# Second attention in another order of quarters, and the convolution's taps moved beside the expert gathers

## The chip, the cores and the metric

One Trainium2 chip, one core. The metric is the device time of one execution in microseconds (us); lower is better. "Before" is the kernel as it stands, "after" the same kernel with the change below.

## The reference, cut to what matters

Two decoder layers on x of 4 batches x 512 tokens x 256 features, float32: attention, cross attention and experts, then again attention, cross attention with modulation, and experts, each with a residual sum and a layer norm.

```python
x = _layernorm(x + _L0_attn_ref(x, ...), axis=-1)
x = _layernorm(x + _L0_xattn_ref(ctx_768, x, ...), axis=-1)
x = _layernorm(x + _L0_ffn_ref(x, L0_ffn_Wr, L0_ffn_W1, L0_ffn_W2), axis=-1)
x = _layernorm(x + _L1_attn_ref(x, ..., L1_attn_pre_proj, L1_attn_post_proj, L1_attn_mem_k, L1_attn_mem_v, ...), axis=-1)
x = _layernorm(x + _L1_xattn_ref(x, ctx_768, ..., L1_xattn_log_dt, L1_xattn_A_re, ...), axis=-1)
x = _layernorm(x + _L1_ffn_ref(x, ...), axis=-1)
```

Two parts are touched. The second attention is causal, has 16 heads and 16 memory keys, mixes its scores over the heads with a 16x16 matrix, keeps of every row of mixed scores only the 64 largest, takes the softmax of them, and mixes over the heads again. The second cross attention holds a state-space convolution, whose kernel ("taps", 512 values for each of 256 channels) depends on weights alone and is computed long before it is used.

## The kernel before, in words

The program is a sequence of blocks; in each, the five engines have instruction streams written out by hand, and wait for one another by semaphores.

**First experts, `l0_experts`.** 39 slots of 128 sorted token rows. For each slot PE makes the hidden values (`hidden`, L1453), transposes the rows of a later slot (L1442) and makes the output (`out`, L1464). DVE copies the slot's first weights (`bring`) and between these computes a piece of the factors of the convolution kernel, `K.V` (32 values a channel) and `K.U` (16 a channel). Four slots make a chunk of 32 channels, 8 chunks in all. Once a chunk, behind `out` of its second slot, PE multiplies the chunk's factors (`taps`, L1473, 32 products of 32x16, tile `f_pk`), and DVE copies the result to `K.taps` in four copies (L1543).

**Combination and norm, `l0_combine_and_norm`.** POOL issues 32 indirect gathers of expert outputs (L2846), eight for each batch. For each batch DVE adds them to x with their gates, takes moments, waits for ACT's root (`root`, L2888) and normalizes x; PE transposes x (`turn`, L2867) and ACT copies it to xT (L2894). Between, PE multiplies the taps with a Fourier matrix in eight steps (`transform`, L2856), each of which ACT copies out (`keep`, L2883); SP stores the eight at the end. Before, the order on PE is four transforms, turn of batch 0, four transforms, turns of batches 1 to 3, and ACT follows it.

**Second attention, `l1_attention`.** The queries of a batch fall into four groups of 128 (quarters); 16 groups in all. Quarter i sees 16 + 128(i + 1) keys at most. `ORDER` says in what order a batch's quarters are worked through. A group is 16 tiles of 8 queries x 16 heads = 128 rows, and two tiles are a pair: 8 pairs a group, 128 pairs in all, numbered k below. Tile r of quarter i is 16 + 128 i + 8(r + 1) wide, so pairs are 24 and 32 wide at the start of the first quarter and 520 and 528 at the end of the fourth. For each pair:

- PE mixes the rows over the heads (`mix`, L1874, tile `a_pmix`); ACT copies that to `mixed` (L1999); POOL adds the causal cut (L2118);
- DVE searches the 64 largest of each row (L2176 to L2260), for a wide row in two halves; its last step signals `found`;
- POOL compares the rows with the 64th value and adds the penalty (`a_probs`, L2141 and L2149); ACT takes the exponentials (L2018) and then the negated maximum of the next pair (`negated`, L2006, `a_negmax`), for which DVE waits before the pair after that;
- DVE inverts the sums (L2215), POOL scales the second mixing matrix (L2102, `a_kp`), and PE multiplies with it in chunks of 128 keys (`post`, L1883, `a_pat`). A tile of over four chunks takes both PSUM banks of `pat`, so that its successor waits for ACT's copies (L2029, L2033). Only the last pair of the fourth quarter has five chunks.

Iteration k of PE is: `mix` of pair k + 2, side work, `post` of pair k - 2, and the products with the values (`heads`, L1901 and L1905, and `output`, L1916) of the group before. ACT's iteration is the copies of mixed scores of pair k + 1, exponentials of k - 1, negated maxima of k, side work, the copies behind `post`, and those of the products. The side work (`l1_units`) hangs on the place of a group in its batch, not on the quarter: at the first place of batch 0 the scores of the group at the second place; at the second place the values (pairs 0 and 1), the scores of the third (pairs 2 to 4) and of the fourth place (pairs 5 to 7, in 3, 3 and 2 units); at the third and fourth place the queries, keys and scores of the next batch. One unit of scores is two heads (L1864, `a_psc`) for one group. A row of over 512 scores is cut in halves of 264, so a unit is four fills of a PSUM bank for the fourth quarter and two for any other (`l1_fills`).

Of the kernel before, what the change touches and what calls it, by code (L numbers as in the profile page):

```python
# [15 lines left out]
B, S, D = 4, 512, 256  # L16
# [945 lines left out]
LO, HI = 32, 16  # L962
MAGIC = 1.5 * 2 ** 23
TWO_PI = 6.283185
CHUNKS = 8
CW = D // CHUNKS
# [409 lines left out]
def l0_experts(nc, G, R, K):  # L1376

    with ExitStack() as ctx:
        sb, ps, sem = buffers(nc, ctx, "f0")
# [10 lines left out]
        px = ps("px", [P, KD, P])  # L1390
        ph = [ps(f"ph{i}", [P, 512]) for i in range(2)]
        py = [ps(f"py{i}", [P, D]) for i in range(2)]
        pk = ps("pk", [LO, CW, HI])
        tapped, taps_read = sem("tapped"), sem("taps_read")
        made = K.steps[0]
        xs_loaded = [sem(f"xs_loaded{i}") for i in range(3)]
        w2_loaded = [sem(f"w2_loaded{i}") for i in range(2)]
        y_stored = [sem(f"y_stored{i}") for i in range(3)]
# [3 lines left out]
        with nc.Block() as block:  # L1402
# [32 lines left out]
            @block.tensor  # L1435
            def _(pe):
                def turn_rows(j):
                    pe.wait_ge(xs_loaded[j % 3], 16 * (j // 3 + 1))
                    if j >= 1:
                        pe.wait_ge(x_ready, j)  # L1440
                    for k in range(KD):
                        ins = pe.transpose(px[:, k, :], xs[:, j % 3, k * P:(k + 1) * P], G.ident[:])  # L1442
                    ins.then_inc(x_turned, 1)

                def hidden(j):
                    pe.wait_ge(x_ready, j + 1)
                    for half in range(2):
                        if j >= 1:
                            pe.wait_ge(h_done, 2 * (j - 1) + half + 1)
                        pe.wait_ge(w1_brought, 2 * j + half + 1)  # L1450
                        for f in range(HF):
                            for k in range(KD):
                                ins = pe.matmul(ph[half][:, f * P:(f + 1) * P], first[half][:, k, f * P:(f + 1) * P], xsT[:, j % 2, k, :],  # L1453
                                                start=(k == 0), stop=(k == KD - 1))
                        ins.then_inc(h_full, 1)

                def out(j):
                    pe.wait_ge(w2_loaded[j % 2], 16 * (j // 2 + 1))
                    if j >= 2:
                        pe.wait_ge(y_done, j - 1)  # L1460
                    for f in range(FT):
                        if f % HF == 0:
                            pe.wait_ge(h_done, 2 * j + f // HF + 1)
                        ins = pe.matmul(py[j % 2][:], hT[j % 2][:, f * P:(f + 1) * P], w2[:, j % 2, f, :],  # L1464
                                        start=(f == 0), stop=(f == FT - 1))
                    ins.then_inc(y_full, 1)

                def taps(c):
                    pe.wait_ge(K.dve_steps, made + K.STEPS * (c + 1))
                    if c >= 1:  # L1470
                        pe.wait_ge(taps_read, c)
                    for i in range(CW):
                        ins = pe.matmul(pk[:, i, :], K.V[:, CW * c + i, :], K.U[:, CW * c + i, :], start=True, stop=True)  # L1473
                    ins.then_inc(tapped, 1)

                turn_rows(0)
                turn_rows(1)
                hidden(0)
                for j in range(SLOTS):
                    if j + 1 < SLOTS:  # L1480
                        hidden(j + 1)
                    if j + 2 < SLOTS:
                        turn_rows(j + 2)
                    out(j)
                    if j % K.PIECES == 1 and 1 <= j // K.PIECES <= CHUNKS:
                        taps(j // K.PIECES - 1)

            @block.scalar
            def _(act):
# [34 lines left out]
            @block.vector  # L1524
            def _(dve):
                def bring(j):
                    e = dve.value_load(R.expert[0:1, j:j + 1], min_val=0, max_val=E0 - 1)
                    for half in range(2):
                        if j >= 1:
                            dve.wait_ge(h_full, 2 * (j - 1) + half + 1)  # L1530
                        w = R.w1[:, bass.ds(e, 1), :, half * 512:half * 512 + 512].rearrange("p a k f -> p (a k) f")
                        dve.tensor_copy(first[half], w).then_inc(w1_brought, 1)

                dve.wait_ge(R.w1_loaded, 16 * E0)
                bring(0)
                for j in range(SLOTS):
                    if j + 1 < SLOTS:
                        bring(j + 1)
                    c = j // K.PIECES - 1
                    if j % K.PIECES == 3 and 0 <= c < CHUNKS:  # L1540
                        dve.wait_ge(tapped, c + 1)
                        for a in range(4):
                            ins = dve.tensor_copy(K.taps[32 * a:32 * a + 32, :, CW * c:CW * c + CW],  # L1543
                                                  pk[:, :, :].rearrange("l c (j a) -> l a j c", a=4)[:, a])
                        ins.then_inc(taps_read, 1)
                    if 0 <= (j - 1) // K.PIECES < CHUNKS:
                        K.piece(dve, (j - 1) // K.PIECES, (j - 1) % K.PIECES)

# [8 lines left out]
GONE = -3e38  # L1557


ORDER = (0, 3, 1, 2)  # L1560
KEYS1 = MEM + S
KK1 = INNER1 // P
CH1 = KEYS1 // P + 1
# [1259 lines left out]
def l0_combine_and_norm(nc, G, R, K):  # L2823

    with ExitStack() as ctx:
# [4 lines left out]
        rstd = sb("rstd", [P, TT])  # L2830
        pf = [ps(f"pf{i}", [P, 512]) for i in range(2)]
        pT = [ps(f"pT{i}", [P, NT, P]) for i in range(2)]
        dft_in, spectrum, kept, stored = sem("dft_in"), sem("spectrum"), sem("kept"), sem("stored")
        moments, rooted, x_ready = sem("moments"), sem("rooted"), sem("x_ready")
        turned, copied, dve_steps = sem("turned"), sem("copied"), sem("dve_steps")
# [5 lines left out]
        with nc.Block() as block:  # L2841
# [9 lines left out]
            def _(pe):  # L2851
# [8 lines left out]
                def turn(b):  # L2860
                    pe.wait_ge(x_ready, NT * (b + 1))
                    for k in range(KD):
                        n = b * KD + k
                        if n >= 2:
                            pe.wait_ge(copied, n - 1)
                        for q in range(NT):
                            ins = pe.transpose(pT[n % 2][:, q, :], G.x[:, b * NT + q, k * P:(k + 1) * P], G.ident[:])  # L2867
                        ins.then_inc(turned, 1)

                pe.wait_ge(dft_in, 16)  # L2870
                for m in range(FT):
                    transform(m)
                turn(0)
                for m in range(FT, 2 * FT):
                    transform(m)
                for b in range(1, B):
                    turn(b)

            @block.scalar
            def _(act):  # L2880
# [9 lines left out]
                def copies(b):  # L2890
                    for k in range(KD):
# [2 lines left out]
                        act.copy(G.xT[:, k, b * S:(b + 1) * S], pT[n % 2][:].rearrange("p a b -> p (a b)")  # L2894
                                 ).then_inc(copied, 1)

                for m in range(FT):
                    keep(m)
                root(0)
                copies(0)  # L2900
                for m in range(FT, 2 * FT):
                    keep(m)
                for b in range(1, B):
                    root(b)
                    copies(b)

# [592 lines left out]
```

## Time and profile before

| | |
|---|---|
| median of 3 runs | 3562.75 us (3560.17 to 3565.22) |
| the profiled execution | 3564.6 us, span 3562.8 us |
| PE busy | 2771.1 us (78%) |
| DVE busy | 2386.4 us (67%) |
| ACT, POOL busy | 1118.4 us, 997.6 us |
| mean granted TensorE clock | 0.823 |

How to read it: the profile covers one execution. The busy share is an average over blocks with different limits; it doesn't tell what a block waits for. PE's clock is granted in two levels, 1.2 and 2.4 GHz, shown as 0.50 and 1.00 of full speed; a number between is a mean over a stretch. Every float32 product shows as two records, so a count of records is twice the count of products. The experts' block runs from 672 to 977 us of the span, the combination to 1032, the second attention to 2586.

### The profile page before, as it was taken

What the parts mean: (1) busy time and instruction counts of PE and PEld (TensorE: products, weight loads), DVE (VectorE), ACT (ScalarE), POOL (GpSimd) and SP (SyncE); (2) the same over time, 40 slices, a digit from 0 to 9 for tenths busy, and PEclk for the clock granted to TensorE, in tenths of its full rate; (3) what the DMA queues carried; (4) which work ended last, traced back from release to release, by engine and by line L of the source; (5) the groups of instructions that cost most, each with busy time, mean ns of one, the idle gap of its engine ahead of it and who ended that gap; (6) DMA issues with size and microseconds to landing.
All of it is one profiled execution on the core that took longest, in us unless ns stands there. A gap on an engine that the chain in (4) does not pass through costs nothing. (4 is left out here: it accounts for less than half of the span.)

```text
span 3562.8 us, 43681 instructions
## 1 busy us (share of the span) xinstructions
PE 2771.1 (78%) x12600; PEld 1905.2 (53%) x12600; DVE 2386.4 (67%) x8897; ACT 1118.4 (31%) x2893; POOL 997.6 (28%) x1242
## 2 busy tenths in 40 slices
PE   4665995499957667767787668765479999999999
PEld 2223564499834345535464445454436656666666
DVE  4996565466334999899989998999767635212112
ACT  1113562244313333433343334332232123222221
POOL 2552000300032454545454545455312210000000
PEclk7556996699976788787867886867679999999999
DMA  2000002455532211212122211111020032212212
GB/s 96 0 0 14 6 1 104 129 170 164 162 131 92 76 59 63 65 65 69 54 72 68 69 55 67 60 54 35 1 93 1 1 89 67 79 53 63 77 51 68
DMA packets 180780, 235.56 MB, mean 66 GB/s; under 512 B 35761, under 2 KB 138869, under 8 KB 180286
## 3 DMA queue, kind: packets, MB, share of 16 engines
q1 hardware_dynamic: 177470, 224.37, 19.7%
q0 software_dynamic: 3072, 8.39, 0.7%
q8 instruction: 103, 1.69, 0.2%
q14 instruction: 135, 1.11, 0.1%
HBM read 170.57 MB, written 62.13 MB: 65 GB/s over the span
## 5 line engine op out<-in xcount | busy, mean ns | idle before, releaser
L1883 PE MATMUL a_pat<-a_kp,a_probs 128*128 128x128 f32 x1344 | 292.8, 392 | 237.7 <-POOL a_kp L2102 232.7
L1883 PEld LDWEIGHTS a_pat<-a_kp,a_probs 128*128 128x128 f32 x1344 | 259.6, 288 | 317.3 <-POOL a_kp L2102 300.0
L2141 POOL TENSOR_SCALAR a_probs<-a_mixed,a_best 128x120 f32<-128x120 f32 (+12 forms) x208 | 302.4, 1454 | 251.8 <-DVE a_best L2208 115.8
L3408 DVE TENSOR_TENSOR tl_hT<-tl_act_out,tl_gate 128x512 f32<-128x512 f32 x128 | 88.6, 692 | 385.8 <-ACT tl_act_out L3279 385.8
L1864 PE MATMUL a_psc<-a_kT,branch 64*128 64x264 f32 (+3 forms) x640 | 225.6, 603 | 119.5 <-ACT a_stage L1966 118.8
L2194 DVE MAX8 a_best<-a_rest 128x8 f32<-128x208 f32 (+23 forms) x768 | 271.2, 374 | 0.0
L2248 DVE MATCH_REPLACE8 a_rest<-a_best,a_rest 128x104 f32<-128x104 f32 (+31 forms) x732 | 266.0, 373 | 0.0
L2102 POOL TENSOR_SCALAR a_kp<-a_kpost,a_rden 128x128 f32<-128x128 f32 x256 | 152.9, 609 | 386.2 <-DVE a_rden L2215 385.8
L1874 PE MATMUL a_pmix<-a_rows,a_kpre 128*128 128x264 f32 (+41 forms) x528 | 185.8, 482 | 84.2 <-ACT a_mixed L1999 79.7
L2186 DVE MATCH_REPLACE8 a_rest<-a_best,a_rest 128x204 f32<-128x204 f32 (+23 forms) x672 | 245.9, 371 | 0.0
L2256 DVE MAX8 a_best<-a_rest 128x8 f32<-128x104 f32 (+31 forms) x732 | 244.6, 377 | 0.0
L3193 PE MATMUL tl_py<-tl_w,tl_hT 128*128 128x256 f32 x1024 | 241.6, 379 | 0.0
L3174 PE MATMUL tl_ph<-xT,tl_w 128*128 128x512 f32 x512 | 240.7, 592 | 0.0
L3193 PEld LDWEIGHTS tl_py<-tl_w,tl_hT 128*128 128x128 f32 x1024 | 194.6, 190 | 80.2 <-issue 60.0
L1864 PEld LDWEIGHTS a_psc<-a_kT,branch 64*128 64x128 f32 x640 | 118.0, 257 | 212.2 <-ACT a_stage L1966 185.9
L2018 ACT ACTIVATE a_probs<-a_probs,a_negmax 128x72 f32<-128x72 f32 (+28 forms) x232 | 126.1, 545 | 262.4 <-POOL a_probs L2149 259.8
L3279 ACT ACTIVATE tl_act_out<-tl_ph,tl_b 128x512 f32<-128x512 f32 x128 | 88.0, 688 | 351.8 <-PE tl_ph L3174 351.8
L2149 POOL TENSOR_TENSOR a_probs<-a_mixed,a_probs 128x72 f32<-128x72 f32 (+28 forms) x232 | 185.3, 820 | 9.3
L1874 PEld LDWEIGHTS a_pmix<-a_rows,a_kpre 128*128 128x128 f32 x528 | 100.3, 226 | 126.1 <-issue 116.1
L1966 ACT COPY a_stage<-a_psc 128x264 f32<-128x264 f32 (+3 forms) x320 | 112.7, 381 | 121.9 <-PE a_psc L1864 115.7
L1453 PE MATMUL f_ph<-f_xsT,xT 128*128 128x128 f32 x1248 | 148.6, 278 | 0.0
L1453 PEld LDWEIGHTS f_ph<-f_xsT,xT 128*128 128x128 f32 x1248 | 147.0, 195 | 1.7
(465 smaller groups left out, 5643.1 us busy)
## 6 DMA issues: line engine op xcount, KB each, us to landing
f_w<-in_L_ffn_W SPq DMA_DIRECT2D x39, 1024.0 KB, 5.7
tl_gate<-l_gates SPq DMA_DIRECT2D x256, 128.0 KB, 2.9
l_scores<-a_stage SPq DMA_DIRECT2D x32, 528.0 KB, 2.7
l_scores<-a_stage SPq DMA_DIRECT2D x32, 400.0 KB, 2.4
l_scores<-a_stage SPq DMA_DIRECT2D x32, 272.0 KB, 2.1
f0o_w<-in_L_ffn_W SPq DMA_DIRECT2D x8, 1024.0 KB, 12.9
sorted_x<-z_blank SPq DMA_DIRECT2D x1, 4992.0 KB, 15.6
f_xs<-sorted_x SPq DMA_DIRECT2D x39, 128.0 KB, 5.3
```

The lines of the kernel that those rows point to most:

```text
L1453: ins = pe.matmul(ph[half][:, f * P:(f + 1) * P], first[half][:, k, f * P:(f + 1) * P], xsT[:, j % 2, k, :], start=(k == 0), stop=(k == KD ...
L1864: full(pe.matmul(out[:, 0:hi - lo], qT[r, j, i * P:(i + 1) * P], kT[r, j, lo:hi], start=True, stop=True))
L1874: ins = pe.matmul(pmix[:, at, 0:hi - lo], kpre[:], rows[:, g % 4, lo:hi], start=True, stop=True)
L1883: ins = pe.matmul(pat[:, at + c, :], probs[:, g % 4, c * P:(c + 1) * P], kp[:, g % 4, :], start=True, stop=True)
L2141: ins = pool.tensor_scalar(p, x, best[:, a, LAST, 7:8], HIDE, ALU.is_lt, ALU.mult)
L2149: pool.tensor_tensor(p, x, p, ALU.add).then_inc(masked, 1)
L2186: last[a, part] = signal(dve.match_replace(values, top, values, GONE))
L2194: ins = dve.max(best[:, a, q, :] if part == 0 else low[:, a, 8 * q + 1:8 * q + 9], values)
L2248: last[a] = signal(dve.match_replace(rest[:, a, 0:wd], best[:, a, q - 1, :], rows_of[a] if q == 1 else rest[:, a, 0:wd], GONE))
L2256: last[a] = signal(dve.max(best[:, a, q, :], rest[:, a, 0:wd]))
L3174: ins = pe.matmul(ph[m % 2][:], lhsT, G.xT[:, k, b * S:(b + 1) * S], start=(k == 0), stop=(k == KD - 1))
L3193: ins = pe.matmul(py[t][:, 0:D], src[:, t * P:(t + 1) * P], w, start=(n == 0), stop=False)
```

## The change

`ORDER` gets the second and the fourth entry swapped. The groups of every batch are now worked through as quarters 0, 2, 1, 3 and not 0, 3, 1, 2. All that is derived from it (widths, stores, fetches, the number of fills of a unit) follows; the places' side work stays. The products of the taps leave the experts' slots and become the first work of PE in the combination's block, with two PSUM tiles in turn; the copies move from DVE to ACT, ahead of the first root. Behind them, PE's order is turn of batch 0, four transforms, turn of batch 1, four transforms, turns 2 and 3; ACT's is the same.

```diff
 l0_experts:
-                def taps(c):
-                    pe.wait_ge(K.dve_steps, made + K.STEPS * (c + 1))
-                    if c >= 1:
-                        pe.wait_ge(taps_read, c)
-                    for i in range(CW):
-                        ins = pe.matmul(pk[:, i, :], K.V[:, CW * c + i, :], K.U[:, CW * c + i, :], start=True, stop=True)
-                    ins.then_inc(tapped, 1)
...
-                    if j % K.PIECES == 1 and 1 <= j // K.PIECES <= CHUNKS:
-                        taps(j // K.PIECES - 1)
...
-                    if j % K.PIECES == 3 and 0 <= c < CHUNKS:
-                        dve.wait_ge(tapped, c + 1)
-                        for a in range(4):
-                            ins = dve.tensor_copy(K.taps[32 * a:32 * a + 32, :, CW * c:CW * c + CW],
-                                                  pk[:, :, :].rearrange("l c (j a) -> l a j c", a=4)[:, a])
-                        ins.then_inc(taps_read, 1)
...
-ORDER = (0, 3, 1, 2)
+ORDER = (0, 2, 1, 3)
...
 l0_combine_and_norm, PE:
+                for c in range(CHUNKS):
+                    if c >= 2:
+                        pe.wait_ge(taps_read, c - 1)
+                    for i in range(CW):
+                        ins = pe.matmul(pk[c % 2][:, i, :], K.V[:, CW * c + i, :], K.U[:, CW * c + i, :], start=True, stop=True)
+                    ins.then_inc(tapped, 1)
+                turn(0)
                 pe.wait_ge(dft_in, 16)
+                pe.wait_ge(taps_read, CHUNKS)
                 for m in range(FT):
                     transform(m)
-                turn(0)
+                turn(1)
                 for m in range(FT, 2 * FT):
                     transform(m)
-                for b in range(1, B):
+                for b in range(2, B):
                     turn(b)
...
 l0_combine_and_norm, ACT:
+                for c in range(CHUNKS):
+                    act.wait_ge(tapped, c + 1)
+                    for a in range(4):
+                        ins = act.copy(K.taps[32 * a:32 * a + 32, :, CW * c:CW * c + CW],
+                                       pk[c % 2][:, :, :].rearrange("l c (j a) -> l a j c", a=4)[:, a])
+                    ins.then_inc(taps_read, 1)
+                root(0)
+                copies(0)
                 for m in range(FT):
                     keep(m)
-                root(0)
-                copies(0)
+                root(1)
+                copies(1)
                 for m in range(FT, 2 * FT):
                     keep(m)
-                for b in range(1, B):
+                for b in range(2, B):
```

The combination's block on ACT, before (`cn_pf` is the transform's PSUM tile, `cn_std` the root, `f0o_w` holds the spectrum):

```order
L2879 UNCONDITIONAL_BRANCH
L2883 COPY f0o_w<-cn_pf 128x256 x4
L2888 ACT_TABLE_LOAD
L2888 ACTIVATE cn_std<-cn_rstd 128x4
L2894 COPY xT<-cn_pT 128x512 x2
L2883 COPY f0o_w<-cn_pf 128x256 x4
L2888 ACTIVATE cn_std<-cn_rstd 128x4
```

and after (`cn_pk` is the taps' PSUM tile):

```order
L2869 UNCONDITIONAL_BRANCH
L2890 COPY f0o_taps<-cn_pk 32x4x32 x32
L2878 ACT_TABLE_LOAD
L2878 ACTIVATE cn_std<-cn_rstd 128x4
L2884 COPY xT<-cn_pT 128x512 x2
L2873 COPY f0o_w<-cn_pf 128x256 x4
L2878 ACTIVATE cn_std<-cn_rstd 128x4
L2884 COPY xT<-cn_pT 128x512 x2
L2873 COPY f0o_w<-cn_pf 128x256 x4
L2878 ACTIVATE cn_std<-cn_rstd 128x4
```

32 copies stand ahead of the first root, and the last four copies of the spectrum now stand ahead of the third root, where they stood ahead of the second.

PE in the second attention where one batch ends and the next begins, before (the last pair of the batch's last group, then the first pairs of the next batch):

```order
L1874 MATMUL a_pmix<-a_rows,a_kpre 128x56
L1874 MATMUL a_pmix<-a_rows,a_kpre 128x64
L1883 MATMUL a_pat<-a_kp,a_probs 128x128 x6
L1874 MATMUL a_pmix<-a_rows,a_kpre 128x72
L1874 MATMUL a_pmix<-a_rows,a_kpre 128x80
L1883 MATMUL a_pat<-a_kp,a_probs 128x128 x8
L1901 MATMUL a_pO<-a_aT_large,a_v 64x128 x6
L1905 MATMUL a_pO<-a_edge,a_v 64x16 x2
```

and after:

```order
L1854 MATMUL a_pmix<-a_rows,a_kpre 128x56
L1854 MATMUL a_pmix<-a_rows,a_kpre 128x64
L1863 MATMUL a_pat<-a_kp,a_probs 128x128 x8
L1854 MATMUL a_pmix<-a_rows,a_kpre 128x72
L1854 MATMUL a_pmix<-a_rows,a_kpre 128x80
L1863 MATMUL a_pat<-a_kp,a_probs 128x128 x10
L1881 MATMUL a_pO<-a_aT_large,a_v 64x128 x8
L1885 MATMUL a_pO<-a_edge,a_v 64x16 x2
```

The narrow mixes of the new batch now stand beside 8 and 10 chunk products and not 6 and 8, and each two heads take 8 products with the values and not 6.

PE at the second place of a batch, pairs 5 and 6, after; the side work there (`a_psc`) is now 12 fills of 264 for each pair, where before it was 6 fills of 400:

```order
L1844 MATMUL a_psc<-a_kT,branch 128x264 x12
L1863 MATMUL a_pat<-a_kp,a_probs 128x128 x6
L1896 MATMUL a_pO<-a_wo,a_cT 128x256 x8
L1897 MATMUL a_pO<-a_bo,a_ones 128x256
L1898 MATMUL a_pO<-x,ident 128x256
L1854 MATMUL a_pmix<-a_rows,a_kpre 128x168
L1854 MATMUL a_pmix<-a_rows,a_kpre 128x176
L1844 MATMUL a_psc<-a_kT,branch 128x264 x8
```

## Rows read from the trace of the kernel before

**Rows 1.** Stretches of the second attention: length, DVE busy, granted clock, DMA
```profile
1086.00:1128.00 42.00, 6.74 (x48) 0.50 0.33 118
1128.00:1468.80 340.80, 338.10 (x1545) 0.77 0.20 66
1468.80:1488.00 19.20, 3.14 (x25) 0.71 0.15 41
```

**Rows 2.** Timeline of the experts: start, duration, engine, work, idle before
```profile
722.35 2.20 PE L1473 MATMUL f_pk<-branch,sk_V 128*32 128x16 f32 x64
...
726.68 0.69 DVE L1532 COPY xT<-f0o_w 128x1024 f32 x1 [4.63 <-PE f_ph L1453]
...
731.83 3.73 PE L1453 MATMUL f_ph<-f_xsT,xT 128*128 128x128 f32 x32
...
739.07 3.73 PE L1453 MATMUL f_ph<-f_xsT,xT 128*128 128x128 f32 x32
...
753.66 2.20 PE L1473 MATMUL f_pk<-branch,sk_V 128*32 128x16 f32 x64
```

**Rows 3.** Timeline of the combination's block
```profile
998.57 0.21 ACT L2888 ACTIVATE cn_std<-cn_rstd 128x4 f32<-128x4 f32 x1
...
1001.61 8.76 PE L2856 MATMUL cn_pf<-f0o_taps,f0o_w 128*128 128x256 f32 x32
...
1017.89 0.20 ACT L2888 ACTIVATE cn_std<-cn_rstd 128x4 f32<-128x4 f32 x1 [3.56 <-DVE cn_rstd L2925]
...
1021.89 3.38 DVE L2916 SCALAR_TENSOR_TENSOR x<-f0o_w,f0o_gates,x 128x256 f32<-128x256 f32 x8 [2.09 <-DMA f0o_w<-sorted_y,f0o_slot]
```

**Rows 4.** Timeline of the second attention's start
```profile
1117.03 7.37 PE L1864 MATMUL a_psc<-a_kT,branch 64*128 64x264 f32 x16
```

**Rows 5.** Timeline, scores of the third quarter at the second place
```profile
1620.50 2.09 PE L1864 MATMUL a_psc<-a_kT,branch 64*128 64x400 f32 x4 [0.63 <-ACT a_stage L1966]
1622.84 2.09 PE L1864 MATMUL a_psc<-a_kT,branch 64*128 64x400 f32 x4 [0.24 <-ACT a_stage L1966]
```

**Rows 6.** Timeline from the third quarter's last search (batch 0) into the next batch
```profile
1468.92 3.32 POOL L2141 TENSOR_SCALAR a_probs<-a_mixed,a_best 128x392 f32<-128x392 f32 x2 [2.81 <-DVE a_best L2208]
...
1472.32 2.00 POOL L2149 TENSOR_TENSOR a_probs<-a_mixed,a_probs 128x392 f32<-128x392 f32 x2
...
1475.26 0.31 DVE L2235 MAX8 a_best<-a_mixed 128x8 f32<-128x40 f32 x2 [6.16 <-ACT a_negmax L2006]
1475.28 2.93 PE L1883 MATMUL a_pat<-a_kp,a_probs 128*128 128x128 f32 x12 [4.01 <-POOL a_kp L2102]
...
1479.74 0.35 DVE L2235 MAX8 a_best<-a_mixed 128x8 f32<-128x56 f32 x2 [4.11 <-ACT a_negmax L2006]
1479.93 3.64 PE L1883 MATMUL a_pat<-a_kp,a_probs 128*128 128x128 f32 x16
...
1485.32 0.23 DVE L2232 TENSOR_REDUCE a_least<-a_mixed 128x1 f32<-128x72 f32 x1 [5.17 <-ACT a_negmax L2006]
```

**Rows 7.** Timeline behind the fourth quarter's last search, batch 1
```profile
1648.22 4.18 POOL L2141 TENSOR_SCALAR a_probs<-a_mixed,a_best 128x520 f32<-128x520 f32 x2 [3.62 <-DVE a_best L2208]
...
1652.48 2.55 POOL L2149 TENSOR_TENSOR a_probs<-a_mixed,a_probs 128x520 f32<-128x520 f32 x2
...
1668.26 1.35 PE L1883 MATMUL a_pat<-a_kp,a_probs 128*128 128x128 f32 x10 [0.94 <-ACT a_edge L2033]
...
1670.13 0.27 ACT L2033 COPY a_edge<-a_pat 128x128 f32<-128x128 f32 x1
```

**Rows 8.** Stretches, as in rows 1: batch 1's fourth, second and third quarter
```profile
1511.10:1648.10 137.00, 135.60 (x585) 0.75 0.20 70
1648.10:1724.70 76.60, 75.78 (x362) 0.83 0.15 44
1724.70:1833.20 108.50, 107.78 (x474) 0.77 0.22 76
```

**Rows 9.** Timeline of the second attention's end
```profile
2566.95 5.85 PE L1883 MATMUL a_pat<-a_kp,a_probs 128*128 128x128 f32 x28 [6.46 <-POOL a_kp L2102]
...
2573.54 0.88 PE L1901 MATMUL a_pO<-a_aT_large,a_v 128*64 128x128 f32 x12 [0.74 <-ACT a_edge L2033]
```

More of the change, by code:

```diff
@@ L1392, in l0_experts @@
         py = [ps(f"py{i}", [P, D]) for i in range(2)]
-        pk = ps("pk", [LO, CW, HI])
-        tapped, taps_read = sem("tapped"), sem("taps_read")
-        made = K.steps[0]
         xs_loaded = [sem(f"xs_loaded{i}") for i in range(3)]
@@ L1538, in _ @@
                         bring(j + 1)
-                    c = j // K.PIECES - 1
-                    if j % K.PIECES == 3 and 0 <= c < CHUNKS:
-                        dve.wait_ge(tapped, c + 1)
-                        for a in range(4):
-                            ins = dve.tensor_copy(K.taps[32 * a:32 * a + 32, :, CW * c:CW * c + CW],
-                                                  pk[:, :, :].rearrange("l c (j a) -> l a j c", a=4)[:, a])
-                        ins.then_inc(taps_read, 1)
                     if 0 <= (j - 1) // K.PIECES < CHUNKS:
@@ L2832, in l0_combine_and_norm @@
         pT = [ps(f"pT{i}", [P, NT, P]) for i in range(2)]
+        pk = [ps(f"pk{i}", [LO, CW, HI]) for i in range(2)]
+        tapped, taps_read = sem("tapped"), sem("taps_read")
         dft_in, spectrum, kept, stored = sem("dft_in"), sem("spectrum"), sem("kept"), sem("stored")
```

## The prediction

> **What bounds the kernel now.** The page gives PE 78% and DVE 67% busy, but the change touches three blocks with different limits, so I read stretches and timelines. I began with the second attention, asking when DVE is idle. Behind the start it is busy 338.1 of 340.8 us [rows 1], and the later batches look the same, so this block lasts as long as DVE's searches, plus the places where DVE idles: the start, where it is busy 6.7 of 42 us, and the begin of every later batch, 3.1 of 19.2 us [rows 1]. The searches of a pair hang on its width alone, so their sum stays. The order can matter only at those idle places, at the end, and where another engine falls behind DVE. In the experts PE is never idle: equal slots follow each other after 7.24 us, and a chunk of four slots with its taps takes 753.66 - 722.35 = 31.31 us [rows 2]. The combination follows the gathers: its last batch starts at 1021.89 as the gather lands [rows 3].
>
> **Taps leave the experts.** Four slots without taps are 4 x 7.24 = 28.97 us, so each chunk gives back 2.34 us: its 64 records (2.20 us, [rows 2]) and what the pipeline loses around them. Eight chunks: **-18.7 us**. Nothing takes the place of it, since PE is the engine that all others wait for there; DVE's copies lie beside PE's work and are worth nothing.
>
> **Taps enter the combination.** Times here are those of before's trace. PE can start at about 979.3, when it waited for the Fourier matrix before. Eight chunks of 64 records at the 2.1 us seen in the experts are 17 us; PE has been idle and starts at the low clock, so I take 19: until 998.3. ACT's four copies a chunk are shorter than PE's chunk and only the last four follow it, 1.2 us. Then the table load and the root: ready at 1001, not at 998.8 [rows 3], 2.2 us late. The four transforms take their 8.8 us [rows 3] behind the first turn, which delays the second root by a little over 1 us. The larger cost is the new place of the second four transforms: turn of batch 1 at 1014, transforms and their copies until 1023, and only then the third root, which stood at 1017.9 [rows 3]. DVE then needs 0.2 us for the reciprocal and 1.6 us to normalize batch 2, and starts batch 3 at about 1025.5, not at 1021.9. **+4 us**. Bounds: 0, if all of it hides behind the last gather; +10, if the taps' products run at the low clock throughout and take 25 us and not 17.
>
> The clock needs a word. In the attention's start PE's granted clock is 0.50, that is 1.2 GHz, for 42 us [rows 1], although scores run there without a pause for 7.37 us at a time [rows 4]. The Trainium skill ("TensorE: Matmul & The Clock Gate", What's actually happening) has it that the low clock is the state of rest and that activity releases the clock; by that, taps and scores would both soon run at 2.4 GHz, the taps' block would be worth +3, and scores at 1.2 GHz over such a stretch would not be seen. Those rows disagree, and so the upper bound stays.
>
> **The order: the start.** In the first four iterations PE makes the scores of the group at the second place, two units each, and DVE waits for it. For the fourth quarter that is 16 records in 7.37 us [rows 4], four times over. For the third it is 8 records; one unit of it follows another after 1622.84 - 1620.50 = 2.34 us at the same clock [rows 5], so 4.7 us. Four times 2.7: **-11 us** (-8 if only columns count, -12).
>
> **The order: the begin of batches 1 to 3.** Three chains hold DVE there [rows 6]. First: the last search, POOL's compare and sum (3.32 + 2.00 us), exponentials, maximum: 6.2 us idle. For the fourth quarter's width POOL takes 4.18 + 2.55 [rows 7], and ACT 0.1 more: +1.5. Second: POOL's scaling, 12 records of `post`, copies: 4.1 us idle. Now 16 records at the same 0.24 us less what overlaps: +0.8. Third: 16 records of `post` for the last pair, 5.2 us idle; now 2 x 10 records, and since five chunks take both banks, the second ten wait for ACT's copies. At the full clock that is 1.35 for ten, 0.94 until the next ten start, 1.35 and 0.8 of copies, 4.4 us [rows 7], no more than the present 3.64 and its copies; at the present 0.228 us a record [rows 6] it is 2 x 2.3 + 2 x 0.8 = 6.2: +1.7, because PE has been idle before. Then two longer heads ahead of the next mix, +0.4. Together 4.4, three times: **+13 us** (0 to +18). What the old order gained back where the fourth quarter ran into the second was nothing: of the second quarter's 76.6 us DVE was busy 75.8 [rows 8], since a search of 8 us covered the chain.
>
> **The order: the second place.** The pairs are shorter for DVE (108.5 / 8 = 13.6 us in the mean, not 137.0 / 8 = 17.1, [rows 8]) and the side work stays or grows: pairs 5 and 6 get 12 fills of 0.92 us (7.37 / 8, [rows 4]) and not 8 as at the old fourth place, 3.7 us more each. Following PE and ACT through pairs 5, 6 and 7, PE ends its iteration some 6.5 us into the next group's first pair, the maximum is ready at 9, and DVE wants it at 7.8. About 1 us for each of four batches: **+4 us** (0 to +15; the upper end if each batch loses what one pair's added fills take).
>
> **The order: the end.** The last group is the fourth quarter: masks +1.5; `post` 16 + 2 x 10 records and not 28 in 5.85 us [rows 9], +1.7, with 1.6 of copies between; in each of eight heads 16 and not 12 records of some 0.06 us (0.88 us for the 12 and a start of 0.2, [rows 9]), +2. **+7 us** (5 to 8).
>
> **Sum.** -18.7 + 4 - 11 + 13 + 4 + 7 = -1.7 us against the profiled execution's 3564.6, which is 1.85 over the median of the runs: 3561 us at the median. A difference of 0.2%, 7 us, is about what a measurement of this kernel can tell from none.
>
> **Rivals.**
> 1. *PE binds at the second place: slower.* The third quarter's pairs leave PE less time, and with the values, 12 fills and the output of the group before it falls behind by more than DVE's queue of mixed rows holds. For it: two of the products there run at the low clock. Against it: at the old fourth place the same pairs with 8 fills leave DVE busy 107.8 of 108.5 us [rows 8]. It decides once PE's iteration of pair 6 ends over 8 us after DVE has begun pair 7. It costs 3 to 4 us a batch more: 3561 + 13 = 3574.
> 2. *The begin of a batch gets no longer: faster.* If PE holds the full clock in `post`, the third chain costs nothing, and if the fourth quarter's longer searches let POOL and PE come in with less left over, the second doesn't either: 3561 - 11 = 3550. Against it: POOL's masks are in the first chain in any case.
> 3. *Taps at the low clock.* +6: 3567.
> 4. *The gain in the experts isn't kept,* for DVE's `bring` becomes the bound: +15: 3576. Against it: DVE is idle 4.6 us ahead of one such copy [rows 2], waiting for PE.
> That the change doesn't do what it says is excluded by the instructions shown above.
>
> **How the numbers follow.** Forecast 0.45, rival 1 0.20, rival 2 0.17, rival 3 0.12, rival 4 0.03, the rest 0.03 without a name. The forecast's own terms are uncertain by some 7 us together (3554 to 3568). The range goes from rival 2 to a little over rival 1: 3550 to 3577. Faster by over 0.2% (under 3555.6): rival 2 and a twentieth of the forecast, 0.21. Slower by over 0.2% (over 3569.9): rivals 1 and 4, and a part of rival 3 and of the forecast, 0.27. Within: 0.52.
>
> **What would show it.** In the profile after: slots of 7.24 us throughout and the experts' block 18.7 us shorter; in the combination the third root late and last; DVE's first dense search some 11 us earlier after the attention's start; at the begin of batches 1 to 3 DVE waits of about 7.7, 4.9, 6.9 and 1 us behind `a_negmax`; under 2 us of DVE waits a batch anywhere else; 32 us from the last search to the block's end and not 25. Waits of DVE in the first pairs of the second quarter of 3 us or more would speak for rival 1, equal waits at the begin of a batch for rival 2.

## The result, and the profile after

The changed kernel takes **3572.19 us** in the median of 13 runs (3565.57 to 3585.64), the kernel before 3560.72 (3554.08 to 3565.51, 13 runs): ratio 1.0031, 95% interval 1.0022 to 1.0040. It is 11.5 us slower, in the upper part of my range (3550 to 3577), where the sum of my terms said -1.7 and I had given no measurable difference the best chance. The profiled execution of the change is the longest of its runs, 3585.6 us; a second one of the same kernel, taken later, took 3571.8. I use both.

From the timelines of both kernels, the length of each stretch in us:

| stretch | before | after | after, second profile | forecast of the difference |
|---|---|---|---|---|
| start of the program to the experts' first product | 672.9 | 674.6 | 668.7 | 0 |
| experts, to the last copy of `f_ys` | 303.6 | 284.5 | 284.7 | -18.7 |
| combination, to the last copy of `xT` | 55.3 | 67.2 | 65.4 | +4 |
| attention, to the first maximum | 54.5 | 53.9 | 53.1 | 0 |
| to the last search's end | 1474.5 | 1490.1 | 1489.5 | +6 |
| to the attention's last `x` copy | 25.1 | 34.9 | 34.9 | +7 |
| to the first `bs_` instruction behind the next attention | 243.4 | 245.2 | 238.1 | 0 |

The combination of the changed kernel, timeline (start, duration, engine, work, in brackets the idle time before and what ended it); what answers to it before is [rows 3]:

```profile
961.34 27.29 PE L2856 MATMUL cn_pk<-branch,sk_V 128*32 128x16 f32 x512 [2.68 <-PEq L1399]
...
988.66 1.05 ACT L2890 COPY f0o_taps<-cn_pk 32x128 f32<-32x128 f32 x4 [2.36 <-PE cn_pk L2856]
989.73 1.28 ACT L2878 ACT_TABLE_LOAD   x1
991.03 0.20 ACT L2878 ACTIVATE cn_std<-cn_rstd 128x4 f32<-128x4 f32 x1
...
991.26 0.18 DVE L2925 RECIPROCAL cn_rstd<-cn_std 128x4 f32<-128x4 f32 x1 [12.29 <-ACT cn_std L2878]
...
994.82 9.21 PE L2838 MATMUL cn_pf<-f0o_taps,f0o_w 128*128 128x256 f32 x32
...
1004.58 0.18 DVE L2925 RECIPROCAL cn_rstd<-cn_std 128x4 f32<-128x4 f32 x1 [6.16 <-ACT cn_std L2878]
...
1014.77 0.18 DVE L2925 RECIPROCAL cn_rstd<-cn_std 128x4 f32<-128x4 f32 x1 [3.25 <-ACT cn_std L2878]
```

The 512 records take 27.3 us, 3.41 us a chunk, where a chunk took 2.20 in the experts [rows 2]. DVE has its moments ready and then waits 12.3, 6.2 and 3.3 us for a root that stands on ACT behind other copies. Batch 3's sum begins at 1016.3, while the last gather was issued at 1001.2, and a gather lands 2.7 us later in the median: the gathers no longer decide.

Stretches of the attention, as [rows 1] and [rows 8] show them before (length, DVE busy, granted clock, DMA): the first quarter's waits, then searches to the end of batch 0, the begin of batch 1, and batch 1's third, second and fourth quarter:

```profile
1080.10:1112.00 31.90, 8.56 (x60) 0.50 0.39 132
1112.00:1454.10 342.10, 336.40 (x1533) 0.75 0.20 67
1454.10:1476.20 22.10, 3.05 (x24) 0.69 0.06 13
1499.90:1610.00 110.10, 107.35 (x474) 0.76 0.23 80
1610.00:1688.70 78.70, 75.75 (x361) 0.85 0.22 66
1688.70:1826.10 137.40, 135.98 (x585) 0.74 0.17 57
```

The third quarter took 108.5 us [rows 8] and takes 110.1; the second 76.6 and takes 78.7; the fourth 137.0 and takes 137.4. The begin of the batch is 19.2 us there [rows 1] and 22.1 here. DVE's waits in it:

```profile
1454.26 4.17 POOL L2121 TENSOR_SCALAR a_probs<-a_mixed,a_best 128x520 f32<-128x520 f32 x2 [3.62 <-DVE a_best L2188]
...
1462.10 0.31 DVE L2215 MAX8 a_best<-a_mixed 128x8 f32<-128x40 f32 x2 [7.65 <-ACT a_negmax L1986]
...
1467.43 0.35 DVE L2215 MAX8 a_best<-a_mixed 128x8 f32<-128x56 f32 x2 [4.95 <-ACT a_negmax L1986]
1467.61 2.50 PE L1863 MATMUL a_pat<-a_kp,a_probs 128*128 128x128 f32 x10
...
1471.04 1.35 PE L1863 MATMUL a_pat<-a_kp,a_probs 128*128 128x128 f32 x10 [0.94 <-ACT a_edge L2013]
...
1474.25 0.23 DVE L2212 TENSOR_REDUCE a_least<-a_mixed 128x1 f32<-128x72 f32 x1 [6.42 <-ACT a_negmax L1986]
```

Against 6.2, 4.1 and 5.2 us in [rows 6]; the forecast said 7.7, 4.9 and 6.9. And where the new waits inside the batch come from, at the third quarter's last two pairs in batch 1:

```profile
1588.02 10.85 PE L1844 MATMUL a_psc<-a_kT,branch 64*128 64x264 f32 x24
...
1598.80 2.93 PE L1863 MATMUL a_pat<-a_kp,a_probs 128*128 128x128 f32 x12
...
1600.55 3.21 POOL L2121 TENSOR_SCALAR a_probs<-a_mixed,a_best 128x376 f32<-128x376 f32 x2 [8.18 <-PE a_pat L1863]
...
1608.78 4.79 PE L1844 MATMUL a_psc<-a_kT,branch 64*128 64x264 f32 x16
1613.50 1.60 PE L1863 MATMUL a_pat<-a_kp,a_probs 128*128 128x128 f32 x12
...
1614.54 3.32 POOL L2121 TENSOR_SCALAR a_probs<-a_mixed,a_best 128x392 f32<-128x392 f32 x2 [5.01 <-PE a_pat L1863]
...
1619.05 0.32 DVE L2240 MAX8 a_best<-a_rest 128x8 f32<-128x152 f32 x1 [1.75 <-POOL a_probs L2129]
```

PE makes 12 score products of the fourth quarter (24 records) in 10.85 us, and only then `post` of the pair two before; then the output, 8 more scores, and the next `post`. POOL's compare writes into one of four buffers of `probs` and waits 8.2 and 5.0 us for these `post` to have read it. DVE's last maximum of a pair overwrites the threshold that POOL's mask of the pair before reads (`masked`); so DVE, now in the second quarter's first pair, waits 1.75 us for POOL. The clock has a part in this: PE is granted 0.50 over the 24 records, and 1.00 where the 16 behind them take 4.79 us. At that rate 24 would take 7.2 us, an estimate, 3.7 less than they do. The end of the block, answering to [rows 9]:

```profile
2577.70 3.78 PE L1863 MATMUL a_pat<-a_kp,a_probs 128*128 128x128 f32 x16 [8.04 <-POOL a_kp L2082]
...
2582.24 2.47 PE L1863 MATMUL a_pat<-a_kp,a_probs 128*128 128x128 f32 x10 [0.77 <-ACT a_aT_large L2009]
...
2585.65 2.47 PE L1863 MATMUL a_pat<-a_kp,a_probs 128*128 128x128 f32 x10 [0.94 <-ACT a_edge L2013]
...
2588.97 1.98 PE L1881 MATMUL a_pO<-a_aT_large,a_v 128*64 128x128 f32 x16 [0.84 <-ACT a_edge L2013]
```

28 records in one piece of 5.85 us [rows 9] have become 36 in three pieces, 10.4 us from the first one's start to the last one's end.

### The profile page after: what moved, and what is told of

Same layout as the page of the kernel before. It is cut to its first block and busy times, and to the rows that moved or that the text cites. A ratio compares the mean times of both kernels' runs of the same rounds, so it can differ in the third digit from the quotient of the medians.

```text
span 3583.8 us, 43675 instructions
## 1 busy us (share of the span) xinstructions
PE 2771.9 (77%) x12600; PEld 1918.5 (54%) x12600; DVE 2377.2 (66%) x8865; ACT 1125.8 (31%) x2925; POOL 994.2 (28%) x1242
## 3 DMA queue, kind: packets, MB, share of 16 engines
q1 hardware_dynamic: 177470, 224.37, 19.6%
## 5 line engine op out<-in xcount | busy, mean ns | idle before, releaser
L1844 PE MATMUL a_psc<-a_kT,branch 64*128 64x264 f32 (+3 forms) x640 | 215.2, 590 | 101.8 <-ACT a_stage L1946 101.0
L2174 DVE MAX8 a_best<-a_rest 128x8 f32<-128x176 f32 (+23 forms) x768 | 271.1, 374 | 0.0
L1854 PE MATMUL a_pmix<-a_rows,a_kpre 128*128 128x256 f32 (+41 forms) x528 | 182.4, 475 | 84.2 <-ACT a_mixed L1979 79.4
L2166 DVE MATCH_REPLACE8 a_rest<-a_best,a_rest 128x172 f32<-128x172 f32 (+23 forms) x672 | 245.6, 370 | 0.3 <-issue 0.3
```

Source lines behind the costliest of these rows:

```text
L1844: full(pe.matmul(out[:, 0:hi - lo], qT[r, j, i * P:(i + 1) * P], kT[r, j, lo:hi], start=True, stop=True))
L1854: ins = pe.matmul(pmix[:, at, 0:hi - lo], kpre[:], rows[:, g % 4, lo:hi], start=True, stop=True)
L2166: last[a, part] = signal(dve.match_replace(values, top, values, GONE))
L2174: ins = dve.max(best[:, a, q, :] if part == 0 else low[:, a, 8 * q + 1:8 * q + 9], values)
```

## The experiments

All medians are beside the kernel before on the same chip. Lines of `a_` instructions stand 20 lower where the taps are beside the gathers, so `L2240` and `L2260` are the same one.

| kernel | median us | before | ratio, 95% interval |
|---|---|---|---|
| order alone | 3580.11 | 3562.49 | 1.0051, 1.0038 to 1.0065 |
| taps alone | 3554.01 | 3562.49 | 0.9978, 0.9969 to 0.9987 |
| order in batch 0 alone | 3558.50 | 3562.49 | 0.9991, 0.9981 to 1.0000 |
| order, units spread | 3560.46 | 3562.49 | 0.9992, 0.9983 to 1.0001 |
| order, units tighter | 3594.50 | 3560.47 | 1.0094, 1.0080 to 1.0109 |
| the change, units spread | 3547.25 | 3560.47 | 0.9968, 0.9955 to 0.9981 |
| taps alone, woven | 3545.80 | 3560.47 | 0.9953, 0.9940 to 0.9966 |
| the change again | 3571.80 | 3560.47 | 1.0035, 1.0023 to 1.0047 |
| woven taps, batch 0 reordered and spread | 3537.04 | 3559.96 | 0.9931, 0.9919 to 0.9943 |
| the change, spread and woven | 3544.81 | 3559.96 | 0.9957, 0.9944 to 0.9970 |

**The two parts apart.** The first theory said that the attention alone makes the change slower. First the order without the taps:

```
-ORDER = (0, 3, 1, 2)
+ORDER = (0, 2, 1, 3)
```

> The order of the quarters alone changed, the taps stay in the experts. Theory A (the attention alone makes the change slower): the stretches of the traces add up to about +25 us in the attention less nothing in the experts, so 3580 to 3586 us, about +20 to +25 against before; the third quarter at the second place shows gaps of about 1.8 us at its third pair and the second quarter at the third place gaps near 3 us a pair. Rival B (most of the loss comes from the taps, which leave the chip's clock low until the attention starts): then this kernel gains from the shorter start of the attention and ends within 5 us of before.

Measured: +17.6 us, a little under the expectation. Of the gaps it named, the second quarter's is there but smaller (78.0 us in batch 1), the third quarter's is not (108.1 us). Then the taps without the order, that is the changed kernel with `ORDER = (0, 3, 1, 2)`:

> The taps alone moved beside the gathers, the order of the quarters as before. Theory A: experts 18 to 19 us shorter, combination about 12 us longer since the 512 small products run at the low clock at about 53 ns each, attention as before: about -7 us. Rival B (the combination's loss depends on the execution, the clock now and then up): -14 us where the products take about 32 ns. Rival C (what is gained before the attention is given back in it): within 3 us of before.

Measured: -8.5 us. In its profile the 512 records take 27.3 us again, the experts are 19.2 us shorter and the combination 67.2 us long, 11.8 more than before. The parts nearly add up: 17.6 - 8.5 = +9.1 us, and the change has +11.5 in one comparison and +11.3 in the other. So the order loses more than forecast (+13) and the taps gain less (-14.7).

**Where the order pays.** Only batch 0 in the new order:

```
+FIRST_ORDER = (0, 2, 1, 3)
+def l1_quarter(n):
+    return (FIRST_ORDER if n < NT else ORDER)[n % NT]
...
-    return n // NT, ORDER[n % NT]
+    return n // NT, l1_quarter(n)
```

> Batch 0 alone in the order first, third, second, fourth; batches 1 to 3 and the taps as in the kernel before. Theory A: the gain at the attention's start (12 us of waits for the scores of the large quarter at the low clock) comes without the price at the begins of batches 1 to 3 and without the one at the end; left are about +4 at the begin of batch 1 and about +4 in the second quarter of batch 0: -3 to -6 us. Rival B (the start's gain comes with the clock, not with the order, and is kept by the next wait): within 2 us of before.

Measured: -4.0 us, with an interval (0.9981 to 1.0000) that just reaches no difference; the profile has to carry the reading. Batch 0's first quarter is 11.6 us shorter, as with the order everywhere, and the price stands behind batch 0 only. Its profile, batch 0 in the new order (first, third, second, fourth quarter), then the first quarter of batches 1 and 2:

```profile
1033.90:1136.70 102.80, 25.97 (x175) 0.65 0.33 105
1136.70:1244.60 107.90, 107.19 (x474) 0.75 0.23 81
1244.60:1323.30 78.70, 75.75 (x361) 0.85 0.21 66
1323.30:1461.20 137.90, 135.94 (x586) 0.74 0.19 65
...
1461.20:1508.70 47.50, 26.09 (x178) 0.78 0.18 49
...
1829.90:1873.70 43.80, 25.96 (x178) 0.69 0.21 59
```

Batch 1's first quarter is 5.2 us longer than before (42.3 us), behind the fourth quarter; batch 2's, behind the third as before, 1.4 us. The end is 24.1 us, not 34.9. So most of the long begin, and the long end, belong to the fourth quarter where it stands last; the 1.4 us of batch 2 are not explained.

**What makes the second quarter wait.** The score units of the fourth quarter stood at pairs 5, 6 and 7 of the second place, as 3, 3 and 2. Spread over four pairs, with the order everywhere and the taps in the experts:

```
-        j = (s - 2) % 3
-        return [("s", NT * b + 2 + (s - 2) // 3, x) for x in ((0, 1, 2), (3, 4, 5), (6, 7))[j]]
+        third, fourth = {2: (0, 1, 2), 3: (3, 4, 5), 4: (6, 7)}.get(s, ()), {4: (0,), 5: (1, 2, 3), 6: (4, 5), 7: (6, 7)}.get(s, ())
+        return [("s", NT * b + 2, x) for x in third] + [("s", NT * b + 3, x) for x in fourth]
```

> As the first of these kernels, with the eight score units of the fourth quarter put at four pairs of the third place's run-up (1, 3, 2, 2) instead of three (3, 3, 2). Theory A (GpSimd's compare waits for the product that frees its probabilities, which stands on TensorE behind these units): 3 to 6 us under the first kernel of this call. Rival B (the units' place doesn't matter, since the fills of the second quarter's own pairs are late): within 1.5 us of it.

Measured: -2.0 us against before (0.9983 to 1.0001, not clear of none), 19.6 under the order alone. Two of the eight units, four products each, stand one pair earlier. That is over three times what I expected. The profiles differ by 16.7 us: in the attention the searches end 9.9 us sooner after the first maximum, and 5.0 lie ahead of the experts, where the two kernels are alike. So the profiles give 9.9 us to the units' place, and not 19.6. Then the opposite:

```
+        third, fourth = {2: (0, 1, 2), 3: (3, 4, 5), 4: (6, 7)}.get(s, ()), {5: (0, 1), 6: (2, 3, 4), 7: (5, 6, 7)}.get(s, ())
```

> As the kernel with the order alone, with the fourth quarter's eight score units later and closer before the fourth quarter (2, 3, 3 at pairs 5 to 7 in place of 3, 3, 2). Theory A (these units' fills, 4 products of 264 columns a head, hold back the products of the weights' transposes, and GpSimd and VectorE wait for those in the pairs just behind): the second quarter's gaps, 2 us a batch in the order-only kernel and none in the spread one, grow to 4 us a batch or more: +6 to +12 us against the order-only kernel. Rival B (the unit that the spread kernel has earlier had to be out of the last pair but one, not fewer overall): within 2 us of the order-only kernel.

Measured: +34.0 us against before, where the order alone had +17.6: 16.4 more (14.4 between the two medians as they stand, which come from two chips), beyond the upper end of 12. Batch 1 of the order alone, in its order (first, third, second, fourth quarter):

```profile
1461.50:1506.10 44.60, 25.95 (x178) 0.81 0.15 40
1506.10:1614.20 108.10, 107.09 (x474) 0.79 0.24 81
1614.20:1692.20 78.00, 75.72 (x361) 0.85 0.22 67
1692.20:1829.60 137.40, 135.97 (x585) 0.74 0.17 57
```

Of the spread kernel the second quarter, and of the tight one the first, third and second:

```profile
1607.00:1682.40 75.40, 75.40 (x361) 0.86 0.20 62
```

```profile
1459.70:1509.30 49.60, 26.03 (x178) 0.70 0.13 36
1509.30:1620.00 110.70, 107.64 (x473) 0.76 0.21 74
1620.00:1701.80 81.80, 75.78 (x362) 0.81 0.22 70
```

DVE's work in the second quarter is 75.4 to 75.8 us in all of them; only its waits go from none over 2.3 to 6.0 us. That is not all that the tight kernel loses. Its searches take 22.7 us more than those of the order alone: 10.2 in the four second quarters, 9.4 at the begins of batches 1 to 3, and the rest mainly in the third quarters. In batch 1's begin the two sets of ten `post` records take 2.50 and 2.47 us, against 1.38 and 1.35 in the order alone, so there the clock stands lower; why is open. The list of waits over the attention's searches names the pair of engines (us in total, times, longest): before, order alone, tight, the change, and the spread kernel.

```profile
DVE a_best L2260 <- POOL a_probs L2149: 0.7, 3, 0.4
```

```profile
POOL a_probs L2141 <- PE a_pat L1883: 91.9, 18, 7.8
DVE a_best L2260 <- POOL a_probs L2149: 6.6, 8, 1.4
```

```profile
POOL a_probs L2141 <- PE a_pat L1883: 96.5, 19, 10.3
DVE a_best L2260 <- POOL a_probs L2149: 19.4, 11, 4.8
```

```profile
POOL a_probs L2121 <- PE a_pat L1863: 106.3, 21, 8.2
DVE a_best L2240 <- POOL a_probs L2129: 14.9, 14, 2.0
```

```profile
POOL a_probs L2141 <- PE a_pat L1883: 94.5, 23, 5.3
```

In the spread kernel's list there is no such wait of DVE. Dose and response fit the chain: scores ahead of `post` on PE, `post` ahead of the compare on POOL, the mask ahead of DVE's last maximum. POOL itself waits about as long in the spread kernel as in the tight one (94.5 and 96.5 us in total), but never over 5.3 us at once. With longest waits of 5.3, 7.8, 8.2 and 10.3 us DVE's waits for POOL are 0, 6.6, 14.9 and 19.4 us: in these four kernels they go with the longest wait and not with the total (before, it is 3.3 and 0.7). The rule is drawn from the four and was not tested apart, and whether more buffers of `probs` would do the same was not tried.

The change itself with the units spread:

> The change whole, with the fourth quarter's score units spread over four pairs. Theory A (the parts add up): before -2 for order with spread units, -8.5 for the taps: 3551 to 3554 us, some 20 us under the change. Rival B (with the taps beside the gathers the attention begins at another phase of the clock and the third quarter at the second place gets its gaps of 2 us a batch back, as the profile of the change has and that of the order alone does not): 3557 to 3562 us.

Measured: 3547.25 us, 25 under the change and better than the sum of the parts, 4 us below the range of the first theory. In its profile the second quarters have no waits and the third quarters 0.8 us in all.

**What the taps cost in the combination.** The forecast took the clock for the risk. Woven order, nothing left out; PE turns a batch as soon as it is normalized, and ACT takes a root in between:

```
 for c in range(CHUNKS):            # tensor
...
+    if c == CHUNKS - 2:
+        turn(0)
-turn(0)
+turn(1)
...
-turn(1)
+turn(2)
...
 for c in range(CHUNKS):            # scalar
+    if c == CHUNKS - 3:
+        root(0)
+    if c == CHUNKS - 1:
+        copies(0)
+        root(1)
```

with the third root ahead of the fourth transform's copy and the fourth ahead of the eighth's.

> The order as before; the taps beside the gathers, but woven with the rest: the first root goes to ScalarE behind five of the eight chunks, TensorE turns the first batch behind seven chunks, the second behind the eighth, the third between the two halves of the transforms. Nothing is left out. Theory A (what the combination lost is VectorE's 12.3, 6.1 and 3.3 us of waits for the roots, which stand on ScalarE behind the copies of the taps and the spectrum): the combination ends where the last gather and 11 us of VectorE, or TensorE's 27 + 16 + 6 us, let it: 10 to 13 us earlier than with the taps moved as in the change, so 3541 to 3545 us. Rival B (TensorE at the low clock is the bound, and what is gained is given back in the attention's start, whose weights and scores are not ready sooner): 3550 to 3554 us.

Measured: -14.7 us against before, 6.2 better than the taps alone, short of the 10 to 13 of the expectation. Its timeline (PE, then DVE):

```profile
958.88 23.80 PE L2856 MATMUL cn_pk<-branch,sk_V 128*32 128x16 f32 x448 [2.68 <-PEq L1399]
...
978.49 0.18 DVE L2928 RECIPROCAL cn_rstd<-cn_std 128x4 f32<-128x4 f32 x1 [2.03 <-ACT cn_std L2879]
...
982.16 3.43 DVE L2917 SCALAR_TENSOR_TENSOR x<-f0o_w,f0o_gates,x 128x256 f32<-128x256 f32 x8 [1.97 <-DMA f0o_w<-sorted_y,f0o_slot]
...
1001.82 3.38 DVE L2917 SCALAR_TENSOR_TENSOR x<-f0o_w,f0o_gates,x 128x256 f32<-128x256 f32 x8 [1.95 <-DMA f0o_w<-sorted_y,f0o_slot]
```

The taps run as slowly as before, 53 ns a record, and yet DVE now waits for the gathers at every batch and the combination lasts 54.3 us, one less than before the change. So the loss came from the place of the roots, and the low clock cost something only through it. (The edit also moves PE's turns; it does not tell the two apart, but the waits of DVE that went are those for the roots.) In the profiles the combination is 12.8 us shorter than with the taps alone. Of these, 2.3 are given back at once: the attention's first maximum comes 56.2 us after the combination, not 53.9, and PE waits 11.0 us there for a DMA, not 9.7. So the second theory of the expectation holds for a small part. Another 4 us by which the two profiles differ lie ahead of the experts, and the profile of the taps alone is 5.7 us over the median of its runs.

**The change again.**

> The changed kernel once more, unedited, for a second profiled execution. Its profile stood at 3585.64 us where the median of its runs was 3572.19. Theory A (its executions differ in where the clock falls in the attention): another profile shows the second and third quarters' gaps smaller, and the sum of the stretches nearer to +10 than to +21. Rival B (the profile is typical and only the runs without a profile are shorter): the same gaps again, 2 us in every third quarter at the second place and 3 in every second one.

Measured: 3571.8 us. The gaps in the second and third quarters are the same to 0.5 us, so the first theory is wrong on the attention. Most of the 13.8 us between the two executions lie outside what the change touches: 6.0 ahead of the experts, 7.1 in the block behind the attention (last section). The combination differs by 1.7.

**Versions that beat both.** The taps woven, batch 0 alone in the new order, its units spread:

> Three edits to the kernel before: the taps beside the gathers and woven with the roots; batch 0 alone in the order first, third, second, fourth; in batch 0 the fourth quarter's score units spread over four pairs. Theory A (the parts add up): -15 for the woven taps, -4 for the first batch, -2.6 for the second quarter's gap of batch 0: 3538 to 3541 us. Rival B (the attention's start, now 19 us earlier, falls at another phase of the clock and loses the 4 us): 3544 to 3548 us.

Measured: **3537.04 us, 23 us under before** (ratio 0.9931, 0.9919 to 0.9943); the parts' own figures (-14.7, -4.0, and the expectation's estimate of -2.6) sum to 21. Against it the change whole, mended in both places:

> The change whole (all four batches in the new order), with the score units spread and the taps woven. Theory A (parts add up): the spread change's 3547 less the 6 us that the weaving gave over what the taps alone gave: 3540 to 3543 us, 1 to 3 us above the kernel with the first batch alone in the new order, since the begins of batches 2 and 3 (+2.4 to +3.9 us each) and the end (+9.8 us) are paid and only the gaps before the large quarters are gained. Rival B (the order's price at begins and end is real but the clock in the block behind gives it back, as it did in the profiles of the order-only and spread kernels, 5 us): at or below that kernel.

Measured: 3544.81 us, 7.8 above it, where I had expected 1 to 3, and not at or below: the order in batches 1 to 3 does not pay. The medians of the last two stand on six runs each, within 17 and 14 us. Their profiled executions are equally long, 3546.7 and 3546.5 us, the first being the longest of its runs. In them the searches take 4.4 us more in the change mended, and the stretch behind the last search 6.6, and the block behind the attention, which is the same work, 7.9 less.

## Why the prediction was wrong

Against the first profile of after, the terms and what they measured:

- **Taps leave the experts, -18.7**: -19.1. Right; no engine took PE's place, and rival 4 is out.
- **Taps enter the combination, +4 (0 to +10)**: +11.8 and +10.1 in the two profiles. *This step failed.* I had counted 2.1 us a chunk, where [rows 2] has 2.20, and had taken the first root to be 2.2 us late, at 1001 in before's times, because I let PE run the taps in 19 us; they took 27.3, over even my bound of 25. With the root behind all of the taps' copies, each of those microseconds went to DVE, and the second and third root came behind it. I did see that ACT's order puts roots behind copies, but charged the third above all. The woven kernel shows that the low clock costs next to nothing where the roots don't stand there: from the experts' end to the attention's first maximum it takes 110.6 us, and before took 109.8. Rival 3 named the cause and not the mechanism.
- **Start, -11**: batch 0's first quarter is 12.2 us shorter. Right.
- **Begins, +13**: 3.5, 3.4 and 3.8 us more in the first quarters of batches 1 to 3, +10.6. Right; the third wait is 6.4 us and not 6.9 because the second ten records ran at the full rate (1.35 us, the first ten 2.50).
- **Second place, +4 (0 to +15)**: +9.8 in the four second quarters and +4.7 in the third ones, +14.5. *This is the other step that failed.* I followed PE to the maximum that DVE wants, that is the chain over the mixed rows and `a_negmax`, which holds six groups. The chain that binds goes over the four buffers of `probs` and comes to DVE through POOL's mask. Rival 1 came nearest: PE was late by more than it asked for, and the second quarter of a batch waits some 3 us in its first pairs, which was its sign; but it too named the queue of mixed rows, and not `probs`. PE's iteration of pair 6 ends, with the output's last product, at 1607.3 us, and DVE began pair 7 at 1595.0, 12.3 us before, where I had put the point at 8. It had 0.20.
- **Fourth quarter last**: 0.3 to 0.9 us more each, +2.0, not forecast.
- **End, +7 (5 to 8)**: +9.8. The masks cost 1.4 (forecast 1.5), `post` and its copies, up to the first head, 11.3 us in place of 6.6, +4.7 (forecast 3.3), and the rest, from there to the last copy, +3.8 (forecast 2), the first heads' 16 records taking 1.98 us and the later ones 1.07. Much of the overrun is the clock: in the tight kernel and in both that have the taps moved and the units spread, the same last stretch takes 30.6 us, +5.5, with ten `post` records in 1.35 us and not 2.47 and the first heads in 1.09. Over `post` the change was granted 0.50. So +7 lies between what the two clocks give.

The sum: -19.1 + 11.8 - 12.2 + 10.6 + 14.5 + 2.0 + 9.8 = +17.4, and with 1.7 ahead of the experts and 1.8 behind the attention the 21 us between the two profiles. The forecast had -1.7 for the same terms. The medians differ by 11.5, since the profile of after was its longest run. Both failures have one form: an engine that is late was followed to one of the waits it feeds, and another came sooner. That the result still fell inside my range is the work of its width, not of the mechanism.

On the clock the forecast had set the trace against a page. The trace kept the upper hand once more: PE, busy without a pause for 27.3 us with the taps (27.29 of 27.70 us), was granted 0.51 of full speed over the stretch.

```profile
961.30:989.00 27.70, 27.29 (x512) 27.21 (x512) 5.30 (x17) 7.42 (x30) 20.62 (x22) 0.51 0.53 174
```

By the Trainium skill ("TensorE: Matmul & The Clock Gate", What's actually happening) activity lifts the throttle; in this stretch the trace does not agree. What it would have given is at most what the experts' 2.20 us a chunk [rows 2] show, at a granted clock of 1.00: 9.7 us less for the taps, most of what the combination lost with the roots where they are.

## What to carry to other kernels

Before moving side work ahead of a product, list every buffer that this product frees and every engine that waits for one, and look at the longest single wait that it causes, not at the total; moving two units of eight by one pair each was worth 10 us here. An instruction of 0.2 us that the bounding engine waits for, such as a root, should stand in its queue where its input is ready, not behind a batch of copies. Judge a reordering by batch: here the gain is had once, at the start, and the price is paid at every begin and at the end.

## What the runs showed of the hardware

Small products at the low clock: the 512 records of 16 columns take 53 ns each in all three kernels looked at, against 34 ns in the experts of the kernel before (2.20 us for 64, [rows 2]). The granted clock is 0.51 over the former and 1.00 over the latter.

The block behind the attention has the same instructions in every kernel and took from 238 to 249 us in the twelve profiles. A short one and the longest, the order alone and the best kernel:

```profile
2602.00:2840.10 238.10, 203.59 (x754) 135.37 (x755) 161.94 (x981) 66.22 (x192) 52.68 (x72) 0.87 0.11 35
```

```profile
2562.10:2811.40 249.30, 213.73 (x754) 138.36 (x755) 162.10 (x981) 66.29 (x192) 52.71 (x72) 0.84 0.10 34
```

PE is busy 203.6 us in the one and 213.7 in the other, for the same 754 records, at a granted clock of 0.87 and 0.84; DVE's and ACT's times are equal to 0.2 us. So a block that an edit does not touch can change by more than some of the effects that this study measures: in the two profiles of the change by 7.1 us. What decides where the clock falls is not shown. The order alone and the change also differ in batch 1: in the order alone the third quarter had no gaps to speak of, in both profiles of the change it had 2 us, with the attention's code the same. The taps' place isn't needed for it: the tight kernel, with the taps in the experts, has the same two waits of DVE for POOL there, 1.8 us together.
